# VectorE instead of ScalarE copies two of the four value products of each batch out of PSUM

## The reference, cut to what matters

```python
q = jnp.einsum('qdh,bcd->bhcq', Q, x) * sq
k = jnp.einsum('qdh,bcd->bhcq', K, x) * sq
v = jnp.einsum('vdh,bcd->bhcv', V, x) * sv
att = jnp.einsum('bhcq,bhCq->bhcC', q, k) / d_query
att = jnp.where(causal, att, -jnp.inf)
p = jax.nn.softmax(att, axis=-1)
y = jnp.einsum('bhcC,bhCv->bhcv', p, v)
z = jnp.einsum('dvh,bhcv->bcd', W, y) * (math.sqrt(d_embed / d_value) / num_heads)
```

## Time and profile before

| what | before |
|---|---|
| device time, median of 3 runs | 1305.89 us (1304.85 to 1306.28) |
| profiled execution, its own time | 1308.45 us |
| its span, first to last instruction | 1306.7 us |
| mean granted TensorE clock | 0.99 |
| busy share of the span: PE, PEld | 95%, 82% |
| busy share of the span: DVE, ACT, POOL | 79%, 77%, 45% |
| `values_out` copies of 128x512 on ACT | 128 |

### The profile page before, as it was taken

The page is one execution under the profiler, slowest core; times in us unless marked ns, Lnnn a source line. Parts: engine busy times, 40 slices in busy tenths (PEclk is TensorE's granted clock), DMA queues, the critical chain, the costliest instruction groups (busy, mean ns, idle before and its releaser), DMA issues.

```text
span 1306.7 us, 38948 instructions
## 1 busy us (share of the span) xinstructions
PE 1245.7 (95%) x11323; PEld 1072.3 (82%) x11331; DVE 1028.3 (79%) x4813; ACT 1006.9 (77%) x3393; POOL 589.8 (45%) x913
## 2 busy tenths in 40 slices
PE   5799987799999999999999999999999999999997
PEld 4688876778788888888888888888888888888885
DVE  6877779977778787778787878788787878787774
ACT  4744448578788888888888888888888888888883
POOL 5811138634344444444444444444444444444443
PEclk9999989989999999999999999999999999999999
DMA  8000000000000000000000000000000000000000
GB/s 215 1 1 0 1 1 1 1 2 2 3 3 9 8 0 8 0 8 0 8 0 8 0 8 0 8 0 8 0 8 0 8 0 8 0 8 0 9 2 18
DMA packets 14303, 11.83 MB, mean 9 GB/s; under 512 B 709, under 2 KB 12522, under 8 KB 14058
## 3 DMA queue, kind: packets, MB, share of 16 engines
q1 hardware_dynamic: 14240, 11.19, 3.2%
q10 hardware_dynamic: 10, 0.00, 0.0%
HBM read 7.00 MB, written 4.19 MB: 9 GB/s over the span
## 4 chain that ended last, share of the span: by engine, by line
PE 88%; DVE 4%; issue 3%; POOL 2%; ACT 2%; DMA 1%; SPq 1%; DVEq 0%; POOLq 0%; ACTq 0%
PE ps L1073 16%; PE ps L1104 14%; PE ps L1087 13%; PE ps L1113 9%; PE ps L1058 6%; PE ps L1059 5%; PE ps L1060 5%; PE ps L1095 2%; PE ps L1094 2%; PE ps L1093 2%; PE ps L987 2%; PE ps L945 1%; PE ps L1005 1%; PE ps L1035 1%; PE ps L1129 1%
## 5 line engine op out<-in xcount | busy, mean ns | idle before, releaser
L776 ACT ACTIVATE pr<-ps,neg_max 128x128 f32<-128x128 f32 (+1 forms) x1024 | 425.9, 431 | 118.6 <-DVE neg_max L520 118.6
L326 POOL TENSOR_TENSOR pr<-pr,rinv 128x256 f32<-128x256 f32 x256 | 157.9, 617 | 555.9 <-DVE rinv L528 555.9
L520 DVE CUSTOM_DVE_ANT_0 ps<-ps,mask 128x128 f32<-128x128 f32 (+1 forms) x1024 | 329.2, 389 | 3.3
L328 POOL TENSOR_TENSOR pr<-pr,rinv 128x512 f32<-128x512 f32 x256 | 266.6, 1041 | 0.0
L535 DVE COPY pT<-ps 128x512 f32<-128x512 f32 x256 | 175.4, 685 | 100.9 <-PE ps L1087 100.9
L776 ACT ACTIVATION_READ_ACCUMULATOR pr<-ps,neg_max 128x1 f32 x1024 | 219.0, 214 | 0.0
L1087 PE MATMUL ps<-ident,pr 128*128 128x128 f32 x1536 | 210.2, 273 | 2.4 <-POOL pr L328 1.1
L1087 PEld LDWEIGHTS ps<-ident,pr 128*128 128x128 f32 x1536 | 179.1, 141 | 21.4 <-POOL pr L328 2.4
L1104 PE MATMUL ps<-pT,space 128*64 128x256 f32 (+1 forms) x2048 | 194.9, 332 | 0.7 <-ACT pT L785 0.5
L1104 PEld LDWEIGHTS ps<-pT,space 128*64 128x64 f32 x2048 | 126.8, 136 | 55.0 <-ACT pT L785 0.7
L1058 PE MATMUL ps<-x_hi,wqk_hi 128*128 128x256 f32 x512 | 168.1, 328 | 3.0 <-issue 2.6
(11 more groups left out here) (171 smaller groups left out, 2582.5 us busy)
## 6 DMA issues: line engine op xcount, KB each, us to landing
out<-x_all SPq DMA_DIRECT2D x16, 256.0 KB, 2.3
x_all<-L_attn_x SPq DMA_DIRECT2D x1, 768.0 KB, 6.1
x_all<-L_attn_x SPq DMA_DIRECT2D x1, 512.0 KB, 4.0
space<-L_attn_Q SPq DMA_DIRECT2D x1, 512.0 KB, 15.6
space<-L_attn_K SPq DMA_DIRECT2D x1, 512.0 KB, 9.8
space<-L_attn_V SPq DMA_DIRECT2D x1, 512.0 KB, 11.6
space<-L_attn_W SPq DMA_DIRECT2D x1, 512.0 KB, 11.9
dft_s<-dft SPq DMA_DIRECT2D x1, 192.0 KB, 2.6
```

Of the source, the lines that this page charges most:

```text
L326: nc.gpsimd.tensor_tensor(pr[:, buf, :, 0, :], pr[:, buf, :, 0, :], r[:, :, 0:1].to_broadcast([P, 2, P]), ALU.mult)
L328: nc.gpsimd.tensor_tensor(pr[:, buf, :, 1:3, :].rearrange("p h b k -> p h (b k)"), pr[:, buf, :, 1:3, :].rearrange("p h b k -> p h (b k)") ...
L520: last = nc.vector.tensor_tensor_reduce(o, o, mask[:, T - w:T], -1.0, -MASKED, ALU.add, ALU.min, neg_max[:, j, 2 * h + qt:2 * h + qt + 1])
L776: last = nc.scalar.activation(dst, ps[:, BANK_S + 2 * j + h, qt * P:qt * P + w], ACT.Exp, bias=neg_max[:, j, at:at + 1], scale=-1.0, accum ...
```

## The change

The copies of the value products with c = 3 (turn 0's step) and c = 1 (turn 6's step, for the next batch) leave ACT's order and enter DVE's. On ACT they stood behind the second head of the exponentials of pair n + 1 and in front of `probs_T(n, 0)`; on DVE they stand behind `qk_low(n + 3, 1)` and in front of `probs_T(n, 0)`. Source, destination and size stay the same, and so does the semaphore `v_ready`, which ACT and DVE now both count up in turn. The copies with c = 0 and c = 2 stay on ACT, and so do the two in front of the first batch. DVE makes 32 copies with c = 3 and 31 with c = 1.

```diff
+            def values_copy(b, j, c):
+
+                dve.wait_ge(v_done, count(4 * b + (c + 1)))
+                nc.vector.tensor_copy(vv[:, j, c % 2, 512 * (c // 2):512 * (c // 2) + 512], ps[:, BANK_X, :]).then_inc(v_ready, 1)
+
...
                     if not (last and p == PAIRS - 2):
                         qk_low(n + 3, 1)
+                    if p == 0:
+                        values_copy(b, jb, 3)
+                    if p == V_TURN and not last:
+                        values_copy(b + 1, 1 - jb, 1)
                     if p + 1 == W_TURN + 2 and not first:
                         add_z(b - 1)
...
                     exp_head(n + 1, 1, 1, pr_of(p + 1))
-                    if p == 0:
-                        values_out(b, jb, 3)
-                    if p == V_TURN and not last:
-                        values_out(b + 1, 1 - jb, 1)
                     probs_T(n, 0)
```

## The result

The changed kernel takes 1336.32 us (median of 6 runs, 1334.85 to 1337.36) beside 1306.40 (6 runs, 1304.85 to 1309.62): ratio 1.022, interval 1.0204 to 1.0235. It is 2.2% slower. The forecast was 1334.7 in a range of 1318 to 1344, slower with a chance of 0.90. The profiled execution took 1336.74 us, forecast 1337.3.

The account below looks back on a forecast made before the run. The bound was PE's own work together with the loop of DVE's maxima, ACT's exponentials and PE's scores. Site 1's 0.33 plus site 2's 0.60 make 0.93 us a batch, 28.8 us over 31 passages: 1334.7 us, range 1318 to 1344.

Parts of the forecast that it names:

- The bound: Whole kernel: a loop of DVE's maxima, ACT's exponentials and PE's scores runs about as long as PE's own work.
- The removal at nothing: ACT, turns 6 and 0: removing the copies (pitch 0.47 us) gains nothing, since ACT then idles until DVE's maxima come.
- The pitch of 0.60: DVE's queue: each moved copy takes 0.60 us until the next instruction starts, as L535 does; bounds 0.47 and 0.68.
- Site 1: Turns 6 to 1: the c = 1 copy makes the maxima 0.60 us later, of which 0.33 us a batch is left.
- ACT's room of 0.27: Site 1, turn 0: ACT had been waiting for PE's products, so only 0.33 of the 0.60 us delay is left.
- Site 2: Turns 0 to 3: the c = 3 copy adds 0.60 us to the maxima, with no room up to turn 3's projection.
- The sum: Both sites together: 0.93 us a batch over 31 passages, 28.8 us, so a median of 1334.7 us, 2.2% slower.
- the signs to look for: Profile after: a new 0.68 us DVE copy, longer ACT idle, turn 1 score set spacing, turn 3 projection gap, PE busy time.

Follow-up runs that it names:

- 8-column copies: The change, but in the loop's 28 batches both DVE copies take 8 columns of 512: 1312.85 us, ratio 1.0037 to the kernel before.
- c = 0: Against the kernel before, only turn 6's c = 0 copy moved from ACT to DVE, right behind z_stats: 1300.09 us, ratio 0.9942.

## Why the prediction was right

- **The bound.** The ring of DVE's maxima, ACT's queue and PE's scores bounds the kernel together with PE's own work. Shown: the same two copies cost 29.9 us in front of the maxima and nothing between them.
- **The removal at nothing.** Right: the idle time behind the copy grew by its pitch, and the 8-column copies gave nothing back. Relief counts only inside the chain, as c = 0 shows.
- **The pitch of 0.60.** Measured 727.30 to 727.90, with a duration of 0.68. The Trainium skill (VectorE: DVE Perf Modes, section The DRAIN you can't avoid) says that the next op waits for an empty pipeline, which would have given 34 us. But the same paragraph adds that a next op that is not held starts earlier, and the prediction left this out when it called the page contradicted. With that sentence the page agrees with the traces, 0.60 us from start to start at a duration of 0.68; it only doesn't say by how much earlier.
- **Site 1.** 0.33 forecast, 0.37 measured. ACT's room of 0.27 was there to the hundredth: `values_out` comes 0.33 late. The other 0.04 arose behind it. ACT's casts and exponentials up to the score sets lasted 0.04 to 0.05 us longer than before (the last exponential 0.50). Why was not tried.
- **Site 2.** 0.60 forecast, 0.59 measured (0.57 in the batches between).
- **The sum.** 0.93 forecast, 0.96 measured a batch, 29.8 us over 31 passages; by the medians 29.9 for 28.8.
- **What was wrong in it.** Of the signs to look for, two were misjudged. PE's busy time was to fall by 6 to 9 us in 300; it fell by 1, because a late start hides in the busy time of the matmul before, which the text itself had said. And the score sets of turn 1 were to stand 1.0 to 1.3 us apart; it is 0.87, because the first set is 0.50 late too, behind the transposes, as the text reckoned elsewhere. The text also named only the exponentials as what the second set waits for. The run with the copies in front of `qk_low` showed that this `qk_low` ends at nearly the same time and takes over when it is moved.

In turn 1, where the prediction read the bound, the wait was probably for `qk_low` all along, in every second batch. ACT's exponentials are complete with the read-out of their sums. In the kernel before, the last one in front of the second score set of turn 7, and that of turn 1:

```profile
717.08 0.24 ACT L776 ACTIVATION_READ_ACCUMULATOR pr<-ps,neg_max 128x1 f32 x1
...
724.66 0.24 ACT L776 ACTIVATION_READ_ACCUMULATOR pr<-ps,neg_max 128x1 f32 x1
```

In turn 7 the set starts at 717.37, 0.05 us behind that read-out's end. In turn 1 it starts at 725.02, 0.12 behind the read-out's end but 0.13 behind `qk_low`'s, at 724.89; and 0.13 is the distance in the run whose profile names `qk_low` as the releaser (715.58 + 0.68 = 716.26, then 716.39). After the change it is 0.13 again (734.74 + 0.69 = 735.43, then 735.56). In the batches between, it is 0.05 behind the read-out. So there are two branches of the ring, the exponentials and `qk_low`, which itself waits for ACT's `qk_high_odd`, and they end within about 0.1 us of each other. The forecast did not suffer, because both stand behind the same delay on ACT: `qk_low` came 0.37 late, like the second set. That the two are so close was not in the reasoning, so this part of the hit is luck. The branch is read from these distances; the profile puts the wait in turn 1 down to ACT, and no run was made for it.

## What to carry to other kernels

When engines wait for each other in a ring, what a moved instruction costs is read at its place: its pitch in the new queue, less the idle time up to the next wait that somebody on the ring needs. The busy shares say nothing on that: 63 copies on the engine with a fifth of its time free cost 30 us at one place and none some 2 us further on, and removing them from the other engine gave nothing where they stood in front of a wait. If a busy PE hides its stalls, count its instructions per stretch instead, or look at the busy time of the weight load.

## What the runs showed of the hardware

How long DVE's `z_norm` lasts (two instructions of 128x128, SBUF to SBUF) goes with whether it starts before or after POOL's scaling of the probabilities. In the kernel before, in every second batch, it started 0.09 us behind POOL and lasted 1.61 us, to 722.41, just past the end of POOL's pair at 722.33:

```profile
720.71 0.62 POOL L326 TENSOR_TENSOR pr<-pr,rinv 128x256 f32<-128x256 f32 x1 [1.11 <-DVE rinv L528]
721.29 1.04 POOL L328 TENSOR_TENSOR pr<-pr,rinv 128x512 f32<-128x512 f32 x1
```
```profile
720.80 1.61 DVE L564 TENSOR_SCALAR z_xn<-x_all,z_mv,z_rstd 128x128 f32 x2 [0.17 <-issue]
```

In the batches between, in the same kernel, it started 0.16 ahead of POOL and lasted 0.89:

```profile
752.36 0.89 DVE L564 TENSOR_SCALAR z_xn<-x_all,z_mv,z_rstd 128x128 f32 x2
```
```profile
752.52 0.64 POOL L326 TENSOR_TENSOR pr<-pr,rinv 128x256 f32<-128x256 f32 x1 [1.01 <-DVE rinv L528]
```

With c = 1 between the maxima it starts ahead of POOL in all batches of the loop but the first and lasts 0.87:

```profile
718.07 0.87 DVE L569 TENSOR_SCALAR z_xn<-x_all,z_mv,z_rstd 128x128 f32 x2
```
```profile
718.23 0.62 POOL L326 TENSOR_TENSOR pr<-pr,rinv 128x256 f32<-128x256 f32 x1 [1.55 <-DVE rinv L528]
```

So in these batches DVE won back 0.7 us right behind a copy of 0.6, and the loss that I had allowed for there didn't come. In the batches between, the copy took idle time: in front of the next probability copy DVE waited 0.73 us for PE before and 0.22 with the copy. POOL's own instructions last 0.62 to 0.64 and 1.04 us in either order, so only DVE is seen to be slowed. All this is read from starts and durations; no run was made for it alone, and what the two engines contend for is not shown.
